# Graph attention on one core: slot sums kept in PSUM, first gathers moved into the sort's block, tile order and sends changed

## The reference

```
qe = q[s] * scale + (edge_attr @ q_rpe_w + q_rpe_b)
ke = k[t] + (edge_attr @ k_rpe_w + k_rpe_b)
ve = v[t] + (edge_attr @ v_rpe_w + v_rpe_b)
compat = einsum('ehd,ehd->eh', qe, ke)
attn = softmax of compat over the edges of one s
out = segment_sum(ve * attn, s)
result = layernorm(x + out)
```

## Time and profile before

| | us |
|---|---|
| median of 3 runs (5312.39 to 5313.63) | 5313.2 |
| the profiled execution | 5311.24 |
| its span, first to last instruction | 5309.5 |
| TensorE busy | 4238.7 (80%) |
| VectorE busy | 4436.5 (84%) |
| ScalarE busy | 3197.7 (60%) |
| POOL busy | 3604.1 (68%) |
| moved by DMA | 756.10 MB |

### The profile page before, as it was taken

The page is one execution under the profiler, slowest core; times in us unless marked ns, Lnnn a source line. Parts: engine busy times, 40 slices in busy tenths (PEclk is TensorE's granted clock), DMA queues, the critical chain, the costliest instruction groups (busy, mean ns, idle before and its releaser), DMA issues. The chain is left out here.

```text
span 5309.5 us, 104472 instructions
## 1 busy us (share of the span) xinstructions
PE 4238.7 (80%) x21888; PEld 3750.4 (71%) x21888; DVE 4436.5 (84%) x18397; ACT 3197.7 (60%) x7799; POOL 3604.1 (68%) x3680
## 2 busy tenths in 40 slices
PE   5658988888888888888888888888888887487875
PEld 4547877777777777777777777777777776366665
DVE  8998988888888888888888888888888886699896
ACT  6986766666666666666666666666666665134444
POOL 0006777777777777777777777777777777556665
PEclk8995555555555555555555555555555555799898
DMA  3104444444444444444444444444444446677774
GB/s 87 31 0 137 144 128 129 129 128 129 129 129 130 128 130 129 128 129 128 129 129 130 129 129 129 129 128 129 128 128 128 129 129 146 236 291 284 288 277 166
DMA packets 377939, 756.10 MB, mean 142 GB/s; under 512 B 142015, under 2 KB 205830, under 8 KB 364984
## 3 DMA queue, kind: packets, MB, share of 16 engines
q1 hardware_dynamic: 254050, 381.31, 25.7%
q0 software_dynamic: 123808, 373.89, 19.7%
HBM read 567.24 MB, written 187.60 MB: 142 GB/s over the span
## 5 line engine op out<-in xcount | busy, mean ns | idle before, releaser
L620 POOL DMA_INDIRECT rec_dram<-recs,place_i x3232 | 3125.3, 967 | 1011.4 <-issue 972.0
L770 PE MATMUL ps_feat<-w_in,edge_in 51*128 51x128 f32 x6464 | 1655.4, 435 | 627.0 <-ACT recs L781 626.6
L770 PEld LDWEIGHTS ps_feat<-w_in,edge_in 51*128 51x128 f32 x6464 | 1436.9, 325 | 802.4 <-issue 712.4
L753 PE MATMUL ps_look<-free_rec,lo_hotT 128*128 128x98 f32 x6464 | 1608.8, 431 | 0.9 <-ACT lo_hotT L794 0.9
L656 DVE SCALAR_TENSOR_TENSOR matches<-ids_b,src_f,ps_const 128x128 bf16<-128x128 int16 (+3 forms) x3232 | 1570.7, 542 | 0.0
L753 PEld LDWEIGHTS ps_look<-free_rec,lo_hotT 128*128 128x128 f32 x6464 | 1472.3, 332 | 1.1 <-ACT lo_hotT L794 1.1
L781 ACT ACTIVATE recs<-ps_feat 128x512 f32<-128x512 f32 x808 | 481.3, 596 | 1482.1 <-DMA rec_dram<-recs,place_i 1478.9
L676 DVE TENSOR_TENSOR place_i<-first,rank 128x4 int32<-128x4 f32 x808 | 132.1, 164 | 709.6 <-ACT recs L781 708.9
L665 DVE CUSTOM_DVE_ANT_0 picked<-hi_hot,ps_look 128x98 f32<-128x98 bf16 x3232 | 631.0, 252 | 0.6 <-PE ps_look L753 0.6
L788 ACT ACTIVATE lo_hotT<-ids_b,minus_p 128x512 f32<-128x512 int16 x808 | 575.1, 712 | 4.3 <-DMA w_in<-kv_dram 4.3
L794 ACT ACTIVATE lo_hotT<-lo_hotT,one 128x512 f32<-128x512 f32 x808 | 570.2, 706 | 0.0
(11 more groups left out here) (170 smaller groups left out, 3583.0 us busy)
## 6 DMA issues: line engine op xcount, KB each, us to landing
ids_b<-id_dram SPq DMA_DIRECT2D x808, 384.0 KB
rec_dram<-recs,place_i POOLq DMA_INDIRECT x3232
edge_in<-in_attr SPq DMA_DIRECT2D x808, 36.0 KB
w_in<-kv_dram SPq DMA_DIRECT2D x808, 12.0 KB
qx_dram<-qx SPq DMA_DIRECT2D x1, 4753.0 KB, 43.9
kv_dram<-dig_i SPq DMA_DIRECT2D x14, 336.0 KB, 2.6
xt<-in_xT SPq DMA_DIRECT2D x14, 224.0 KB, 3.3
qx_t<-qx_dram,node_i POOLq DMA_INDIRECT x98
```

What stands on the lines that cost most here:

```text
L620: pool.indirect_dma_start(rec_dram[:, :], bass.IndirectOffsetOnAxis(place_i[j][:, m:m + 1], 0), recs[j][:, m, 0:ROW], None).then_inc(scatt ...
L753: last = nc.tensor.matmul(ps_look[j % NS][:, m, 0:NB], lo_hotT[j % NS][:, P * m:P * (m + 1)], free_rec[j % 2][:, :], start=True, stop=True)
L770: last = nc.tensor.matmul(ps_feat[j % 2][:, m, :], edge_in[j][0:K_ROWS, tile], w_in[j][0:K_ROWS, :], start=True, stop=True)
```

## The change

- The folded sums `acc` are columns 256 to 319 of the same PSUM bank that `ps_sum` is, instead of an SBUF tile.
- The tiles come in the order `RANK_OF`: ranks 97, 96, 95, then 0 to 94. Tiles of 26, 27 and 27 slots stand ahead of that of 67; the last has 28.
- At the end of the sort's block POOL waits for `qx_out` and for the ranking, issues the node gathers of six tiles, then waits for the scatters and gathers the records of the first tile. The node rows and that tile's records lie in memory that `qx` had.
- The groups end with lengths 7, 7, 6, 4, 2, 2 instead of 14, 8, 4, 2: eleven instead of nine. `ready_at` gives one tile an iteration up to 83, two up to 97, then all that are ready. The loop is four iterations shorter.
- ScalarE copies prob_s before it adds to the denominators. It loads Exp before the loop and Sqrt after the last softmax; the last two roots load nothing.
- The seven helper tiles are computed only in the branch. The two opening matmuls take the bf16 `iota_row` instead of the fp32 `ident`.

```diff
+AHEAD = RB + 2
+RANK_OF = [NB - 1, NB - 2, NB - 3, *range(NB - 3)]
...
+        T["qx"] = kept("qx", [P, NB, QX])
+        T["qx_ring"] = [T["qx"][:, k, :] for k in range(QB)]
...
-            for j in range(NU):
-                pool.wait_ge(scattered[j], 16 * CT * (NCH // NU))
...
             both_ways(pool, send_loop)
+            pool.wait_ge(qx_out, 16)
+            pool.wait_ge(order_steps, RANKED)
+            for b in range(AHEAD):
+                pool.indirect_dma_start(T["qx_ring"][b], None, qx_dram[:, :],
+                                        bass.IndirectOffsetOnAxis(node_i[:, RANK_OF[b]:RANK_OF[b] + 1], 0)).then_inc(T["qx_in"][b], 16)
+            for j in range(NU):
+                pool.wait_ge(scattered[j], 16 * CT * (NCH // NU))
+            pool.wait_ge(T["qx_in"][0], 16)
+            pool.indirect_dma_start(T["rec_0"][:, 0:SLOTS[RANK_OF[0]], :].rearrange("p s f -> p (s f)"), None, rec_dram[:, :],
+                                    bass.IndirectOffsetOnAxis(T["qx_ring"][0][:, QX - 1:QX].bitcast(I32), 0)).then_inc(T["rec_in_0"], 16)
...
+        slots = [SLOTS[t] for t in RANK_OF]
...
-        acc = [sb(f"acc{i}", [P, DIM]) for i in range(2)]
...
+        acc = [t[:, SUM, :] for t in ps_sum]
...
-        marks = [*range(0, NB - 14, 14), NB - 14, NB - 6, NB - 2, NB]
+        marks = [*range(0, NB - 28, 14), NB - 28, NB - 21, NB - 14, NB - 8, NB - 4, NB - 2, NB]
-        last_step = NB + 10
+        last_step = NB + 6
...
+        ready_at = {b: [] for b in range(-1, last_step)}
+        ready = 0
+        for b in range(last_step):
+            for _ in range(1 if b < NB - 14 else 2 if b < NB else NB):
+                if ready < NB and groups[group_of[ready]][1] + 3 <= b:
+                    ready_at[b].append(ready)
+                    ready += 1
...
-            for b in range(ahead):
-                gather_node(b)
-                if b >= ahead - RB:
-                    gather_rec(b - (ahead - RB))
+            for b in range(1, RB):
+                gather_rec(b)
...
-                nc.tensor.matmul(ps_lg[i][:, :, :], ident[:, :], ident[:, :].unsqueeze(1).broadcast_to((P, H, P)), start=True,
+                nc.tensor.matmul(ps_lg[i][:, :, :], iota_row[:, :], iota_row[:, :].unsqueeze(1).broadcast_to((P, H, P)), start=True,
...
-                dve.tensor_reduce(acc[i][:, :], ps_sum[i][:, 0:SUM, :].rearrange("p s f -> p f s"), AX.X, ALU.add).then_inc(whole, 1)
+                dve.tensor_reduce(acc[i], ps_sum[i][:, 0:SUM, :].rearrange("p s f -> p f s"), AX.X, ALU.add).then_inc(whole, 1)
...
-                act.activation(den[b % RB][:, :], den[b % RB][:, :], ACT.Identity, bias=tiny[:, 0:1]).then_inc(den_safe, 1)
                 if b >= 2:
                     act.wait_ge(pool_spent, b - 1)
                 act.activation(prob_s[i][:, :, 0:k], ps_prob[i][:, :, s - k:s], ACT.Copy).then_inc(prob_copied, 1)
+                act.activation(den[b % RB][:, :], den[b % RB][:, :], ACT.Identity, bias=tiny[:, 0:1]).then_inc(den_safe, 1)
...
-                act.activation(warmed[:, :], tiny[:, 0:1], ACT.Exp)
+                if groups[g][1] + 1 < NB - 1:
+                    act.activation(warmed[:, :], tiny[:, 0:1], ACT.Exp)
...
+            act.wait_ge(consts_set, 3)
+            act.activation(warmed[:, :], tiny[:, 0:1], ACT.Exp)
...
+                    if b + 1 == NB - 1:
+                        act.activation(warmed[:, :], tiny[:, 0:1], ACT.Sqrt)
```

More of the change, by code:

```diff
@@ L110, in gnn_kernel @@
         )
+        T["qx"] = kept("qx", [P, NB, QX])
+        T["qx_ring"] = [T["qx"][:, k, :] for k in range(QB)]
+        first = max(SLOTS[t] for t in RANK_OF[::RB])
+        T["rec_0"] = T["qx"][:, QB:NB, :].rearrange("p b f -> p (b f)")[:, 0:first * ROW].rearrange("p (s f) -> p s f", f=ROW)
+        T["qx_in"] = [keep.enter_context(nc.semaphore(f"qx_in{k}")) for k in range(QB)]
+        T["rec_in_0"] = keep.enter_context(nc.semaphore("rec_in0"))
         digits = keep.enter_context(ExitStack())
@@ L935, in attend_stage @@
 def attend_stage(nc, T, rec_dram, qx_dram, out):
-    iota_p, iota_f, ident, base, deg, more = (T[k] for k in ("iota_p", "iota_f", "ident", "base", "deg", "more"))
+    iota_row, iota_p, iota_f, ident, base, deg, more = (T[k] for k in ("iota_row", "iota_p", "iota_f", "ident", "base", "deg", "more"))
     ranked_deg, node_i, crowded = (T[k] for k in ("ranked", "node_i", "crowded"))
@@ L999, in attend_stage @@
         ps_sum = [pb(f"ps_sum{i}", [P, 2 * SUM, DIM]) for i in range(2)]
+        acc = [t[:, SUM, :] for t in ps_sum]
         ends, consts_set, opened = (sem(n) for n in ("ends", "consts_set", "opened"))
[L1002 to L1003 removed]
+        rec_in = [rec_in_0] + [sem(f"rec_in{r}") for r in range(1, RB)]
         y_out = [sem(f"y_out{k}") for k in range(3)]
@@ L1033, in group_at, with overflow @@
         def group_at(b):
-            for g, (_, b1) in enumerate(groups):
-                if b == b1 + 1:
-                    return g
-            return None
-        def ready_at(b):
-            found = []
-            for b0, b1 in groups:
-                late = b - (b1 + 3)
-                if b1 < NB - 2 and 0 <= late < b1 - b0:
-                    found.append(b0 + late)
-                elif b1 >= NB - 2 and late == 0:
-                    found.extend(range(b0, b1))
-            return found
+            return next((g for g, (_, b1) in enumerate(groups) if b == b1 + 1), None)
+        ready_at = {b: [] for b in range(-1, last_step)}
[5 more added lines that the diff above has]
+                    ready += 1
+        assert ready == NB
         def by_head(t):
             return t.rearrange("p (h d) -> p h d", h=H)
-        def overflow(eng, loop):
+        def overflow(eng, loop, after=None, before=None):
             m = eng.value_load(crowded[0:1, 0:1], min_val=0, max_val=1)
             with eng.If(m > 0):
+                if before:
+                    before()
                 passes = eng.alloc_register(f"passes_{loop.__name__}")
@@ L1058, in overflow @@
                     loop(b, passes)
+                if after:
+                    after()
         def every_pass(eng, b, passes, one):
@@ L1131, in _ @@
                     gather_rec(b + RB)
-                    gather_node(b + ahead)
+                    gather_node(b + AHEAD)
             for k in range(3):
@@ L1138, in edge @@
             def edge(b):
-                i, s = b % 2, SLOTS[b]
+                i, s = b % 2, slots[b]
                 lg = ps_lg[i][:, :, 1:s + 1]
@@ L1278, in residual @@
                     dve.wait_ge(y_out[y_part(b)], y_turn(b))
-                dve.tensor_tensor(y[:, b % YB, :], acc[b % 2][:, :], qx[b % QB][:, DH:DH + DIM], ALU.add).then_inc(added, 1)
+                dve.tensor_tensor(y[:, b % YB, :], acc[b % 2], qx[b % QB][:, DH:DH + DIM], ALU.add).then_inc(added, 1)
             def group(g, k):
@@ L1316, in _ @@
                 if b < NB:
-                    i, s, own = b % 2, SLOTS[b], SLOTS[b] - on_pool[b]
+                    i, s, own = b % 2, slots[b], slots[b] - on_pool[b]
                     half = own // 2
```

75 lines of the change are left out of this document (40 added, 35 removed).

## The result

The changed kernel takes 5173.1 us, median of 4 runs (5170.2 to 5176.3), against 5312.8 of the kernel before beside it: ratio 0.9738, interval 0.9721 to 0.9755, 139.7 us less. I had predicted 5193, 120 less, within 5165 to 5238. The profiled execution took 5176.3 us, its span 5174.6.

What follows compares the result with a forecast made beforehand. Bound: VectorE's attend-stage periods, stretched by two instructions waiting for POOL's product. T(97) = 4584.4 + 675.8 - 120.3 + 5 + 3 + 9 + 10 + 5 - 3 = 5168.9; + 20.4 + 1.7 = 5191.0, against the median 5193; range 5165 to 5238.

Steps and rivals of the forecast that it cites:

- The slot sums in PSUM: Attend stage, VectorE: scale and residual, with one SBUF operand each, no longer wait for POOL's product; -120.3 us.
- Start: From the sort's end to the 67-slot fourth tile's maximum, T(3): release at 4558, first dot about 4562.5, T(3) at 4584.4.
- Tiles held by TensorE: Attend stage: some ten tiles of 46 and more slots held 0.3 to 0.5 us by TensorE; +5 us.
- Chance meetings: Attend stage, elsewhere: allowance for chance meetings of full engines; +3 us, bounds 0 and 20.
- Groups: Layer norm groups: nine roots ahead of the last tile instead of six stalls, 3.0 us each; +9 us.
- Cold TensorE: Tile after each root: slower sums on cooled TensorE no longer hidden by the period, 9 x 1.1; +10 us, bounds 0 and 16.
- Sends: From iteration 85 POOL sends two a tile; seven or eight tiles exceed VectorE by 1.3 us, half taken back; +5 us.
- ScalarE's order: prob_s copied ahead of the den step saves 0.2 us in 15 tiles of up to 31 slots; -3 us.
- Tail: From the last tile's maximum, T(97), to the end of the span: 20.4 us, against 38.5 before.
- The full queue: Rival: transfers hold tiles; 5201 at 379 GB/s, 5218 by the 358 GB/s rule, 5252 at 305; chance 0.25 (5200 to 5252).
- The lower clock: Rival: a fuller TensorE stays at the lower clock in the attend stage, some 5569 us; chance 0.04.
- That one SBUF operand beside a PSUM output is held: Rival: VectorE's waits stay; start, tail, roots and sends alone count, -15, about 5298 us; chance 0.04.

Runs made afterwards that it cites:

- the undone kernel: The changed kernel with acc put back from PSUM into an SBUF tile; ratio 1.0023 (1.0013 to 1.0032) to the kernel before.
- the combined kernel: The changed kernel with VectorE's group step one iteration later, marks every 7 tiles, fewer double sends, first gathers back in the attend stage; 5151.2 us, ratio 0.9695.
- the run with den first: The changed kernel with ScalarE's old order, the den step ahead of the copy of prob_s; 134.5 us saved against the kernel before.
- the first three experiments: acc in PSUM alone in the kernel before (ratio 0.9804); the changed kernel with acc back in SBUF (1.0023); the changed kernel with scaled sums in SBUF (17.1 us saved).
- PSUM alone: The kernel before with one edit, acc in PSUM beside the slot sums; ratio 0.9804 (0.9788 to 0.9820), 122.9 us less.
- the gathers in the stage: The changed kernel with all node gathers and the first record gather back in the attend stage; 141.4 us saved against the kernel before.

## Why the prediction was right, and where its terms were off

The forecast of 5193 was 20 us above the result, its mechanism right. The large term came out to a tenth of a microsecond; the small ones around it were mostly too high, and their errors don't cancel. Step by step, each period compared with that of the same rank before, less the time by which the two instructions were stretched in it:

- **The slot sums in PSUM, -120.3**: -120.4 in the changed kernel, -120.7 in the periods of the kernel with that edit alone. Shown. A PSUM result was taken to cost 0: the fold takes 423 ns with acc in PSUM and 415 in the undone kernel, under 1 us over 98 tiles.
- **Start, T(3) = 4584.4**: 4589.7. The sort ended 2.4 us later in this execution. VectorE began 8.5 us after the end of the last issue, between my 5.5 and 9.6 and 1.1 later than I took, which a quicker set-up took back. The rest, 3.1, is two dots that waited 1.4 us each for records and TensorE's opening tiles: I had costed the records as there in time. My sum took the early gathers and never weighed them against leaving them in the stage; the combined kernel beside the changed one shows that they cost 2.9.
- **Tiles held by TensorE, +5**: -1.4 in tiles 3 to 15. The step that failed is TensorE's 1.3 + 5.51 = 6.8 for 48 slots: the sums begin inside the edge matmuls' recorded time, so the overlap was counted twice. From edge matmul to edge matmul TensorE took 6.56 in that tile, no more than the 6.54 that I had for VectorE, and the tile's period was 6.53. **Chance meetings, +3**: -0.4.
- **Groups, +9**: the nine root tiles have 28.4 us of excess, the six of before 18.5, so +9.9.
- **Cold TensorE (sums at the lower clock behind a root), +10**: +8.0 in the eight tiles behind roots, late sends included. **Sends, +5**: outside those only +0.9, in tile 91. Two sends a tile fill POOL, but its lag from tile 88 on (2.4, 3.8, 5.2, 6.6 us behind the maximum) reached VectorE only there before the next root cleared it.
- **ScalarE's order, -3**: -6.3 in tiles 42 to 85, of which the run with den first gives 4.0 to the order, and -0.9 from tile 88 on. The step was too narrow: den is waited for in tiles of up to 37 slots, not only of up to 31. The remainder is in alternate tiles that ran 0.2 to 0.4 us longer before.
- **Tail, +20.4**: 20.1.
- **T(3) to T(97), 584.5**: 564.8. The terms behind the main edit came to +29 and measured +9.7 (564.8 - 675.8, plus the 120.7 by which the two instructions were stretched in the 94 periods).

Three slips changed none of this: 94 x 3.0 is 282 and not 285, the records of the 67-slot tile would by their sum have landed at 4574.6 and not 4576, and tile 41 had two neighbours below 7 us, 6.90 and 6.23; tile 43 was undisturbed like it (5.57).

**Rivals.** The full queue falls: 370 GB/s went through 50 us and 352 to 357 through whole slices without holding a tile, where a ceiling of 305 would have given 5252. The rule of about 358 GB/s (the Trainium skill, SBUF — State Buffer, Summary: rules for kernel authors) would have given 5218; a stretch of 50 us passes it by 3%, and the result is 45 us below that estimate. The lower clock falls: 0.94 is granted on average in the stage, and it is at the lower level only at the start, at the end and behind the roots. That one SBUF operand beside a PSUM output is held falls with the first three experiments.

## What to carry to other kernels

A tiny VectorE instruction that takes microseconds and ends together with GpSimd's tensor instruction, and has two SBUF inputs, is waiting for GpSimd; giving it one input in PSUM took 120 us off here and cost under 1. Which of several such instructions is held depends on when GpSimd's instruction is released, so moving the copy that releases it by 0.2 us cost 21 us. A stall that a slow period hid is worth a second look once the period is short: consuming the root one iteration later gave 23 us from T(3) to the end, all edits beside the main one some 17. And work put ahead of a block's end has to be weighed against the later release of all engines.

## What was not expected of the hardware

- The hold goes by the release of POOL's product, up to 0.7 us before its recorded start and while POOL is still issuing a gather; the switch lies between 0.090 and 0.095 us.
- From the end of POOL's last issue in the block to VectorE's first instruction of the next it took 9.6 us in the kernel before, 8.5 in the changed one, 7.2 in the combined one and 13.9 behind an early gather of 67 slots. On the chips where the ranking ends late it was 12.3 with PSUM alone and 13.3 with the gathers in the stage; there VectorE, with the ranking, is the last to leave the block.
- Work ahead of a block's end is not free for waiting there: against the combined kernel it delayed the release of all engines by 10 us and saved 8.6 us of waiting at the first tile.
- TensorE's sums last 6.84 us behind a stall of 3.25 us and 4.48 without; the clock was granted at 0.50 behind the stall. Deferring the root removed both.
